# First attention of a two-layer tower: q and k in two fp32r parts, scores on row halves of PE, values and result in one SBUF buffer

## The reference

```python
h = tok(x)                                       # (8, 512, 256)
h = h + L0_attn(layernorm(h)); h = h + L0_ffn(layernorm(h))
h = h + L1_attn(layernorm(h)); h = h + L1_ffn(layernorm(h))
# L0_attn: 16 heads of 16 features
Q, K, V = (proj(W) for W in (W_Q, W_K, W_V)); Q, K = rope(Q), rope(K)   # x * cos + x_flip * sin
scores = jnp.where(causal, einsum('bhsd,bhtd->bhst', Q, K) / 4, -jnp.inf)
out = einsum('bhst,bhtd->bhsd', softmax(scores), V) @ W_O.T
```

## Time and profile before

| what | us |
|---|---|
| median of three runs (1912.12 to 1915.68) | 1915.01 |
| the profiled execution | 1910.06 |
| its span in the trace | 1908.2 |
| busy in the span: PE, DVE, ACT, POOL | 1335.6, 1011.3, 635.0, 721.1 |
| mean granted clock of PE, share of full speed | 0.863 |

### The profile page before, as it was taken

The page is one execution under the profiler, slowest core; times in us unless marked ns, Lnnn a source line. Parts: engine busy times, 40 slices in busy tenths (PEclk is TensorE's granted clock), DMA queues, the critical chain, the costliest instruction groups (busy, mean ns, idle before and its releaser), DMA issues. The chain is left out here.

```text
span 1908.2 us, 32827 instructions
## 1 busy us (share of the span) xinstructions
PE 1335.6 (70%) x9797; PEld 1053.7 (55%) x9798; DVE 1011.3 (53%) x1870; ACT 635.0 (33%) x1271; POOL 721.1 (38%) x596
## 2 busy tenths in 40 slices
PE   0466646999999746534442399646699699999997
PEld 0255533555555544323331267534689578888886
DVE  0688854666767274557778255463544233333332
ACT  0032222565656412223221044212234234333342
POOL 6166662555554001113445500200174135444454
PEclk9788776999999878867766599867799899999999
DMA  1023337999998000023323254022001363444431
GB/s 28 18 77 111 112 114 154 246 252 256 244 255 227 7 6 0 0 61 110 110 78 100 64 113 92 10 83 76 10 25 33 120 216 55 115 113 115 112 55 26
DMA packets 161663, 190.87 MB, mean 100 GB/s; under 512 B 27028, under 2 KB 137052, under 8 KB 161604
## 3 DMA queue, kind: packets, MB, share of 16 engines
q1 hardware_dynamic: 133044, 129.24, 24.6%
q0 software_dynamic: 28560, 60.91, 12.7%
HBM read 112.89 MB, written 78.25 MB: 100 GB/s over the span
## 5 line engine op out<-in xcount | busy, mean ns | idle before, releaser
L1122 DVE TENSOR_REDUCE att_top<-att_psA 128x2 f32<-128x1024 f32 (+8 forms) x256 | 245.3, 986 | 186.4 <-PE att_psA L998 118.5
L1092 ACT ACTIVATE att_prob<-att_psB 128x512 f32<-128x512 f32 (+4 forms) x464 | 231.7, 536 | 137.4 <-PE att_psB L1017 71.3
L2175 POOL DMA_INDIRECT out<-ffn1c_y,ffn1c_table x72 | 114.2, 1585 | 179.8 <-ACT ffn1c_y L2288 106.0
L997 PE MATMUL att_psA<-att_ka,att_qa 96*128 96x384 bf16 (+3 forms) x512 | 126.3, 312 | 31.5 <-POOL att_mask_kNone L913 30.3
L1016 PE MATMUL att_psB<-att_qa,att_ka 98*128 98x256 bf16 (+3 forms) x512 | 128.0, 303 | 4.7 <-ACT att_prob L1092 2.2
L1050 PE MATMUL att_psO<-att_prob,att_vu 128*32 128x128 f32 (+7 forms) x1408 | 106.0, 405 | 35.1 <-ACT att_prob L1092 35.0
L2316 DVE TENSOR_TENSOR ffn1c_hid<-ffn1c_psG,ffn1c_sil 128x512 f32<-128x512 f32 x72 | 49.8, 691 | 144.4 <-PE ffn1c_psG L2216 144.4
L2216 PE MATMUL ffn1c_psG<-ffn1c_w_h,ffn1c_xh 128*128 x288 | 97.8, 421 | 10.8 <-DMA ffn1c_w_l<-experts_lo 3.8
L998 PE MATMUL att_psA<-att_mask_qNone,att_idb 128*128 128x128 bf16 x512 | 101.7, 226 | 0.0
L2164 POOL DMA_INDIRECT ffn1c_rows<-normed_rows,ffn1c_table x72 | 70.9, 984 | 78.0 <-DVE ffn1c_gate L2336 53.8
L1050 PEld LDWEIGHTS att_psO<-att_prob,att_vu 128*32 128x32 f32 x1408 | 51.1, 109 | 85.7 <-issue 64.1
(11 more groups left out here) (365 smaller groups left out, 3742.8 us busy)
## 6 DMA issues: line engine op xcount, KB each, us to landing
prep_raw<-in_w_all POOLq DMA_DIRECT2D x27, 512.0 KB, 6.9
experts_hi<-prep_hi POOLq DMA_DIRECT2D x27, 512.0 KB, 3.6
experts_lo<-prep_lo POOLq DMA_DIRECT2D x27, 512.0 KB, 4.3
ffn1c_w_h<-experts_hi SPq DMA_DIRECT2D x8, 1536.0 KB, 6.8
ffn1c_w_l<-experts_lo SPq DMA_DIRECT2D x8, 1536.0 KB, 11.0
qkv_near<-near_keys SPq DMA_DIRECT2D x32, 320.0 KB, 4.4
v_rows<-qkv_vaug SPq DMA_DIRECT2D x8, 1024.0 KB, 4.6
att_vu<-v_rows SPq DMA_DIRECT2D x32, 256.0 KB, 3.7
```

Of the source, the lines that this page charges most:

```text
L997: pe.matmul(out, q, ka[0:KROWS, u.buf, h, 0:cols], start=True, stop=True)
L1092: act.activation(dst, src, ACT.Exp, scale=0.25).then_inc(s["exp"], 1)
L1122: dve.tensor_reduce(dst, src, AX.X, ALU.max).then_inc(s["max"], 1)
L2175: pool.indirect_dma_start(out=rows_out, in_=y[:, t.buf, :], in_offset=None, out_offset=bass.IndirectOffsetOnAxis(ap=table[:, t.value:t.val ...
```

## The change

`project_rope` handles single tiles instead of sequences: all its buffers hold two tiles, ACT normalises (with a per-token scale and shift), and q and k are split into two fp32r parts instead of three bf16 terms. v stays in SBUF, in `va`, with features outside and heads inside and a row of ones; the columns of W_V and the rows of W_O are permuted for it. `attend_pairs` is new and serves the first layer. Each of two row halves of PE has one head: 16 rows high, 16 rows remainder, 16 rows high again, against k's high, high, remainder. The mask is added to the A scores only, in two 64-row parts; the exponentials' triangle on the diagonal is cleared by POOL (`affine_select`). A and B share a ring of three double banks. B runs three units after A (before two), the values one after B, and the division one after that. The result overwrites the values in `va`. The pieces of the split weights are no longer tied to PE; one stands ahead of the four selects in each of POOL's rounds.

```diff
@@ project_rope @@
+            for m in range(NT):
+                if m + 1 < NT:
+                    turn(m + 1)
+                pe.wait_ge(s["xTl"], m + 1)
+                if m >= 2:
+                    pe.wait_ge(s["rot1"], m - 1)
...
+                mm.then_inc(s["v"], 1)
+                if m >= 1:
+                    turn_back(m - 1)
+            turn_back(NT - 1)
...
-            pool.tensor_tensor(part[:, 1], rest[:], one[:].unsqueeze(2).to_broadcast([P, 4, S]), ALU.mult).then_inc(s["m"], 1)
-            pool.tensor_tensor(part[:, 2], rest[:], part[:, 1], ALU.subtract).then_inc(s["l"], 1)
...
@@ attend_pairs: POOL @@
+            for u in range(NU + 3):
+                if u < n_pieces:
+                    piece(pool, u)
+                v = u - 3
+                if 0 <= v < NU:
+                    for j, through in enumerate((2, 4, 5, 6)):
+                        tri = prob[:, v % 2, :, START[j]:START[j] + P]
+                        pool.wait_ge(s["exp"], 6 * v + through)
+                        pool.affine_select(out=tri, in_=tri, compare_op=ALU.is_ge, fill=0.0, base=0,
+                                           pattern=[[0, HG], [1, P]], channel_multiplier=-1).then_inc(s["tri"], 1)
@@ attend_pairs: PE @@
+            def bank_free(kind, v, n):
+                at = place[kind, v, n]
+                if at >= RING:
+                    before, w, m = order[at - RING][1:]
+                    pe.wait_ge(s["max" if before == "A" else "exp"], 6 * w + m + 1)
+                return at % RING
+            def query_scores(u, n):
...
+                i = (0, 1, 2, 2, 3, 3)[n]
+                cols = P * (i + 1)
+                for q in (range(2) if n < 2 else (n % 2,)):
+                    for g in range(2):
+                        r = slice(64 * g, 64 * g + QROWS)
+                        pe.matmul(psS[:, bank, g, col:col + cols], qa[r, u % LOADED, q, P * i:P * (i + 1)],
+                                  ka[r, u % LOADED, q, 0:cols], start=True, stop=True, tile_position=(64 * g, 0),
+                    for part in range(2):
+                        for g in range(2):
+                            mm = pe.matmul(psS[:, bank, g, col + cols - P:col + cols], half[r, part, :], shut[r, part, :],
...
+            def values(w, j):
+                pe.wait_ge(s["tri"], TG * w + j + 1)
+                if j == 0 and w >= 1:
+                    pe.wait_ge(s["outT"], w)
+                for h in range(HG):
+                    mm = pe.matmul(psO[VW * h:VW * h + DK + 1, P * j:S], va[:, TG * b + j, :, HG * hg + h],
+                                   prob[:, w % 2, h, START[j]:START[j] + S - P * j], start=(j == 0), stop=(j == TG - 1),
+                                   tile_position=(0, VW * h), skip_group_check=True)
...
+            for u in range(NU + 5):
+                for n in range(6):
+                    if u < NU:
+                        query_scores(u, n)
+                    if 0 <= u - 3 < NU:
+                        key_scores(u - 3, n)
+                    if n == 1 and 0 <= u - 1 < NU:
+                        turn_top(u - 1)
+                    if 1 <= n <= TG and 0 <= u - 4 < NU:
+                        values(u - 4, n - 1)
+                    if n == 3 and 0 <= u - 5 < NU:
+                        turn_out(u - 5)
@@ attend_pairs: ACT @@
+            def exps(v, n):
+                if n == 0 and v >= 2:
+                    act.wait_ge(s["pv"], v - 1)
+                j = (0, 0, 1, 1, 2, 3)[n]
...
@@ attend_pairs: DVE @@
+            dve.memset(psO[:], 0.0).then_inc(s["clear"], 1)
+            for at in range(LOADED):
+                for g in range(2):
+                    dve.memset(ka[64 * g + 32:64 * g + 64, at].bitcast(F32), -1.0).then_inc(s["minus"], 1)
@@ split_experts @@
-        def load(n, par):
-            pool.wait_ge(s_unit, n)
-            pool.dma_start(raw[:, par, :], raw_dram[n]).then_inc(s_raw[par], 16)
+    def load(pool, n):
+        pool.dma_start(raw[:, n % 2, :], raw_dram[n]).then_inc(s_raw[n % 2], 16)
```

554 lines of the change are left out of this document (361 added, 193 removed).

## The result

The changed kernel takes 1921.99 us (median of 20 runs, 1916.7 to 1927.0), the kernel before in runs beside it 1915.75 (20 runs, 1910.4 to 1919.8). The ratio is 1.0035, with a 95% interval of 1.0024 to 1.0046: 6 us slower, where 84 us faster was predicted, and outside the range of 1796 to 1878. The profiled execution took 1921.2 us, its span is 1919.4, 11.2 more than before.

The account below looks back on a forecast made before the run. It took the rotary stage as bound by its loop through the engines and the attention by PE; 1908.2 less 63 and 18 gave a span of 1827, said as 1832 us, range 1796 to 1878.

Parts of the forecast that it names:

- rival 4: Attention: PE's clock falls as PE stands still once per round; at a round of 15 us, 1989 us in all; chance 0.03.
- PE's work at full clock: Attention, a full round: values, transposes, score products and masks on PE sum to 6.0 us paired, 9.0 unpaired.
- the chance of 0.16: Attention: weight loads that don't overlap, a round of 10.3 us (1852 us in all), together with rival 5's unchanged 10.4 us round.
- the ring's formula: Attention: lags through the shared three-slot ring set a round of 8.8 to 9.2 us paired, 10.3 with loads not overlapped.
- The start: Attention: PE starts 13.5 us in, behind DVE's twelve memsets (11 us) and two more copies; before 8.8.
- The rotary stage: First layer's attention input stage: the loop through the engines takes 3.9 us per tile, 143 us against 206.2, 63 saved.
- rival 3: Rotary stage: the loop runs at POOL's and DVE's slow forms, 5.0 us per tile, 1867 us in all; chance 0.08.
- POOL's floor: Attention: the weight piece (6.6 us) and four selects (2.5) keep a round from going under 9.3 us.
- PE waits for the select before the first value product: Attention: sign expected in the trace each round, since the select stands behind POOL's piece; standstill up to 2 to 3 us.
- The unit for the round trip: Attention: one further unit for the maxima's round trip can give at most 1.6 us; taken as nothing.
- The row halves: Attention: two heads' score products run at once, 2.1 us per round instead of 4.3; sign: pairs start almost together.
- The price of a change of tiling: Attention: switching PE's tiling costs at most 0.1 us each, ten per round instead of two, at most 0.8 us more.

Follow-up runs that it names:

- the control: The changed kernel run again unaltered, beside other runs of the kernel before: ratio to the kernel before 1.0035.
- e10: The changed kernel with the first query-side score product issued four times and the second key-side one three times per round: ratio to the kernel before 0.9653.
- e16: e12 with POOL's piece of the split weights behind the four selects instead of ahead of them: ratio to the kernel before 0.9486.
- e3: The changed kernel with the further unit for the maxima's round trip through DRAM taken away, all second-pass distances one less: ratio to the kernel before 1.0006.
- e4: The changed kernel with the four groups of value products at one place of the round instead of four steps: ratio to the kernel before 0.9911.
- e15: e12 with 90 transposes of the identity on PE while it waits for the first loads: 1812.7 us, ratio to the kernel before 0.9469.
- e17: e15 with query-side score products three times in the three rounds that have maxima alone: 1810.7 us, ratio to the kernel before 0.9456.
- e18: e14 with the first query-side product issued eight times in place of three: ratio to the kernel before 0.9773.
- e2: The changed kernel without the causal mask products of the query side: ratio to the kernel before 0.9805.
- e14: e12 without the query-side mask products and with the first query-side product three times instead of four: 1837.8 us, ratio to the kernel before 0.9597.
- e12: The changed kernel with ACT's copy one step earlier, first query-side product four times, and mask copies ahead of the first loads: ratio to the kernel before 0.9498.

## Why the prediction was wrong

**The clock (rival 4, chance 0.03).** The largest error. The prediction named the mechanism and its place, and then set it aside with "a slow clock fills PE's time, after which these rows have it high again". The half sentence is true and the conclusion false: it is high again for 6.7 us and low for 20.4. The step that failed is this one, that a lost clock was left out of the sum. The other argument, PE busy 80% at a clock of 0.90 in the earlier trace rows, was drawn from another mixture of work; in this attention PE had gaps of 1.63 us in 10.47 at full clock, busy 84%, and lost it. The price was also framed wrongly, as all or nothing (a round of 15): the mean of the mixture is 13.5. From the first copy on, 26 rounds took 352.8 us; at 10.47 they take 272.2: **81 us** for the clock. In the control the same sum is 70 us, since its clock held once for 30 us, and e10 gives that back: its attention is 356.9 us from first product to last copy, the control's 425.5.

**PE's work at full clock.** 6.0 us predicted (7.6 with loads that don't overlap), 8.3 measured. The wrong term was the score products, 2.1 us where 4.0 are needed. I had taken the pairs at half of the sum, and had 3.7, for weight loads that don't overlap, as a case within the chance of 0.16; the 0.10 us over per pair fit that case. The round at full clock was 10.47 instead of 9.6; 29 rounds, **25 us**. With weights not overlapped the ring's formula gave 10.3, close to 10.47; a part of that is luck, since it has no term for ACT's copy, a gap of 0.71.

**The start.** 17.8 us instead of 13.5. The path was another. SP's loads stood behind the first two memsets of k's buffers only (the first load is issued at 204.59, the twelve memsets end at 216.4), not behind 11 us for all. The two mask copies, which the prediction named, are queued behind sixteen loads, and the second lands 6.6 us after its issue at 212.69; this wait had no term. 4 us, and 1 in the light rounds, where PE waited 3.18 us for the fourth unit's loads:

```profile
240.44 0.48 PE L1267 MATMUL att_psS<-att_ka,att_qa 48*128 48x128 f32 x2 [3.18 <-DMA att_ka<-k_parts]
```

Sum of the attention: 81 + 25 + 5 = 111 of the 115 us between 341 and 456.

**The rotary stage.** 63 us saved predicted, 93 measured. The loop was the right one, its terms too long: the sum of the rotary parts at 0.68 in place of up to 1.09, and neighbours on one engine start some 0.1 us before the end of the one ahead (0.48 for a cast of 0.59, 0.51 for an affine step of 0.60), which I had added at full length. 3.15 us a tile instead of 3.9. The slow forms of rival 3 didn't occur.

**POOL's floor.** Selects at 0.637 us (predicted 0.62), the piece 6.3 us (predicted 6.6): both right, and without effect on the round (e10, e16). "PE waits for the select before the first value product" was wrong; the values come a unit behind the exponentials, so the selects have a round of slack. PE waited for ACT's copy there, which the prediction didn't name.

**The unit for the round trip.** Predicted at nothing. Without it (e3) the kernel is 0.3% faster than the change, with overlapping intervals: near nothing.

**The row halves.** They do run together, with starts 3 to 4 ns apart, as the prediction's sign had it, but a pair of 512 columns takes 0.34 us against 0.47 one after the other: a factor of 1.4, not 2. The Trainium skill ("TensorE: Matmul & The Clock Gate", Part 3) says that products in distinct row groups run at the same time; the trace agrees. The price of a change of tiling was bounded by 0.8 us a round, and that bound doesn't follow: it takes 5120 columns for the 32 value products of the earlier trace rows, which at a mean of 320 have 10240, and four at once would need 1.1 of the 2.29 us. In e4, which removes six of the ten changes, it can't be told from the change of clock, so it wasn't measured.

The two large errors meet in one place. Halving an engine's work was priced as time saved. Here it also opened the gaps that cost the clock, and the term that should have been compared with the rest was PE's work **at full clock** against the round that the other engines dictate.

## What to carry to other kernels

When a change shortens the busiest TensorE's work, add up its work at 2.4 GHz and set it against the round that the other engines dictate; where new gaps appear, price a lost clock as a case of its own with a real chance, as a mixture of both levels. A TensorE that is busy 95% at a granted clock of 0.6 is not the bound to be relieved: look for the one or two gaps per round at full clock, take them away by order (a copy one step earlier gave 2.7%), and fill what is left with repeats that release nothing late (3.8% by itself). Both with the earlier mask copies save 101 us against the kernel before, 0.9498 of its time; a busy start on top (e15, e17) is not distinguishable. Check the granted clock after each such edit, since e18 shows that added work doesn't always bring it back. Try removals of TensorE work only together with a look at the clock: without the masks the kernel was faster while the clock went to and fro (e2), and 21 to 25 us slower once it was held (e14 against e16 and e15).

## What the runs showed of the hardware

- More work made the kernel faster: 1939.7 to 1892.4 us by six more pairs of small products per round, and less work made it slower in e14 and faster in e2. Where the clock was lost it went to and fro between the levels 1.2 and 2.4 GHz, in the change in step with two rounds (27.3 us).
- Equal busy shares of PE in the profile (0.96) went with granted clocks of 1.00 (e12) and 0.79 (e18). The idle time of a full-clock round was alike too in e10 and e18 (0.6 us). Which work keeps the clock can be read from neither.
- Two products of fp32r on the two row halves, 48 or 50 rows deep, with fresh weights each, start 3 to 4 ns apart: 0.34 us per pair of 512 columns, 0.28 of 384, 0.12 to 0.21 of 256.
- An affine select of 128x512 in float32 on POOL takes 0.637 us.
